# Attention reads its keys and values from a DRAM buffer of batch rows instead of by one gather per batch and source

## The reference, cut to what matters

```python
# x: 128 batches x 32 tokens x 256, that is 4096 tokens
x = x + ffn0(cond0(x))      # cond0: one of 200 matrices of 32x32 per batch; ffn0: 8 experts, top 2, low-rank terms
x = x + ffn1(attention(x))  # ffn1: 2 experts, top 1, hidden 1024

# attention: 8 heads in 4 groups, head size 32, paged cache of 4112 blocks of 16 positions
q, k, v = project(x); q, k = rope(rms(q)), rope(rms(k))
slot = pos // 16; off = pos % 16; blk = table[batch, slot]     # pos = kv_len + token
k_blocks[blk, :, off, :] = k;  v_blocks[blk, :, off, :] = v    # all batches write first
k_all = k_blocks[table]                                        # then all batches read
allowed = (kpos <= pos) & (kpos > pos - 128)                   # a window of 128 keys
o = softmax(where(allowed, q @ k_all.T / 16, -inf)) @ v_all
attention = o @ Wo.T
```

## Time and profile before

| what | value |
|---|---|
| median of 3 runs | 1223.65 us (1211.5 to 1227.43) |
| the profiled execution, its own time | 1226.37 us |
| its span, first to last instruction | 1224.6 us |
| PE / DVE / ACT / POOL busy | 945.7 / 721.4 / 535.9 / 559.1 us |
| mean granted clock of PE | 0.962 |
| moved by DMA | 130.04 MB |

### The profile page before, as it was taken

How to read it: one execution, slowest core, us unless ns; L and a number is a source line. 1 busy time by engine, 2 the same in 40 slices (tenths; PEclk the granted TensorE clock), 3 DMA queues, 4 the chain that set the end, 5 groups by cost and what they waited for, 6 DMA issues and landing times.

```text
span 1224.6 us, 21749 instructions
## 1 busy us (share of the span) xinstructions
PE 945.7 (77%) x4475; PEld 698.1 (57%) x4476; DVE 721.4 (59%) x2742; ACT 535.9 (44%) x1733; POOL 559.1 (46%) x558
## 2 busy tenths in 40 slices
PE   1896600789993766639988888888886999999995
PEld 1895400556662322218866677666774666767664
DVE  4225670344443899968978788878884444444442
ACT  0231000122221433329978787878783433333331
POOL 0001775050003777546777777777762122222221
PEclk9999999999997988968999999999997999999998
DMA  6766224874336644312222222222221111111110
GB/s 167 272 209 178 106 102 173 314 232 130 120 119 242 182 139 141 107 45 66 68 69 73 63 70 73 67 70 70 70 75 47 38 51 52 48 47 43 50 36 26
DMA packets 93174, 130.04 MB, mean 106 GB/s; under 512 B 28729, under 2 KB 77419, under 8 KB 91808
## 3 DMA queue, kind: packets, MB, share of 16 engines
q0 software_dynamic: 33872, 68.94, 18.9%
q1 hardware_dynamic: 44688, 42.02, 10.8%
q10 hardware_dynamic: 14576, 18.65, 5.0%
HBM read 98.37 MB, written 55.38 MB: 126 GB/s over the span
## 4 chain that ended last, share of the span: by engine, by line
PE 42%; issue 19%; POOL 19%; DMA 9%; DVE 8%; DVEq 1%; ACT 1%; SPq 0%; POOLq 0%; ACTq 0%
POOL kvring L417 12%; PE bank L839 9%; PE bank L851 9%; POOL slots_in L421 7%; PE bank L723 6%; PE bank L652 3%; DMA kvring<-written_blocks,read_i 2%; DMA work<-in_x 2%; PE bank L715 2%; PE bank L860 2%; PE bank L663 2%; DMA work<-slots_in 1%; DVE work L1153 1%; PE bank L731 1%; PE bank L770 1%
## 5 line engine op out<-in xcount | busy, mean ns | idle before, releaser
L421 POOL DMA_INDIRECT slots_in<-rows,slot_i x96 | 98.6, 1027 | 152.0 <-DVE slot_i L980 102.9
L417 POOL DMA_INDIRECT kvring<-in_cache,read_i x128 | 137.4, 1073 | 49.9 <-issue 36.0
L417 POOL DMA_INDIRECT kvring<-written_blocks,read_i x128 | 137.9, 1077 | 41.4 <-issue 40.8
L770 PE MATMUL bank<-work,kvring 88*128 88x256 f32 x512 | 136.0, 388 | 0.9 <-issue 0.8
L417 POOL DMA_INDIRECT work<-slots_out,slot_i x64 | 72.4, 1132 | 126.7 <-DMA slots_out<-work 102.4
L839 PE MATMUL bank<-experts,work 128*128 x264 | 126.4, 601 | 0.6 <-ACT work L621 0.6
L851 PE MATMUL bank<-experts,work 128*128 x528 | 124.9, 379 | 1.8 <-DVE work L1252 1.8
L851 PEld LDWEIGHTS bank<-experts,work 128*128 128x128 f32 x528 | 100.1, 190 | 43.2 <-issue 32.9
L421 POOL DMA_INDIRECT out_x<-work x33 | 33.2, 1007 | 191.2 <-DVE work L1264 178.4
L582 ACT ACTIVATE work<-work 128x176 f32<-128x176 f32 x256 | 110.3, 433 | 7.3 <-DVE work L1205 5.6
L1247 DVE TENSOR_TENSOR work<-bank,work 128x512 f32<-128x512 f32 x66 | 45.7, 692 | 106.4 <-ACT work L629 106.4
(11 more groups left out here) (235 smaller groups left out, 2016.2 us busy)
## 6 DMA issues: line engine op xcount, KB each, us to landing
slots_in<-work ACTq DMA_DIRECT2D x8, 1152.0 KB, 5.1
work<-slots_in SPq DMA_DIRECT2D x72, 128.0 KB, 2.1
slots_out<-work SPq DMA_DIRECT2D x72, 128.0 KB, 1.7
...
```

Source lines behind the costliest of these rows:

```text
L417: pool.indirect_dma_start(dst, None, src, bass.IndirectOffsetOnAxis(ap=index, axis=0), **kw).then_inc(done, 16)
L421: pool.indirect_dma_start(dst, bass.IndirectOffsetOnAxis(ap=index, axis=0), src, None, **kw).then_inc(done, 16)
L770: mm = pe.matmul(bank[6 + q // 2 % 2][:, (q % 2) * 256:(q % 2) * 256 + 256], kv[q][:, r * 256 + KW:r * 256 + 2 * KW], pt[q % 2][:, r * 256 ...
```

## The change

- **A buffer in DRAM.** Each group ("unit") of 8 batches gets a tensor `kv_rows` of 8 x 176 rows of 1 KB. `stage_cache(u)` gathers 88 whole blocks of 16 KB of the cache into one of two halves of `kvring`; `write_rows(u)` stores them. All 16 units are done in the first expert stage (`PRE2 = 16`), on POOL, unit `u` not before the share `u / 17` of the 72 tiles is done. They stand where the first 16 batch gathers stood, ahead of the gathers of the QKV stage.
- **The patch.** When the QKV stage has drained, `stage_copies(u)` gathers those of the 88 blocks that a batch has written to from `written_blocks`, and `write_copies(u)` scatters them over the buffer: four units at once, then one for each 8 batches, 32 batches ahead.
- **The read.** SP loads, for each batch, 160 consecutive rows (80 x 2 KB) from the buffer, starting at an offset that it reads into a register, into a ring of 16 batches in `work`. A window now has 160 keys and not 176.
- **PE.** Scores: four products, one for each group, 32 rows deep, 64 columns of weights, 160 columns (L837), in place of two of 128 x 128 x 176. Values: eight products with 32 columns of weights and 64 columns (L868) in place of two with 128 and 256. The keys of two batches are turned and copied together. The probabilities' turn is as before but for 80 in place of 88.
- **ACT and DVE.** ACT copies the turned probabilities (was DVE) and the output of a tile at once; the spreading of queries, the distance and the key copy leave it. DVE copies the keys of two batches at once, builds the mask in one instruction, and takes the minimum of scores that were scaled by -1/16 in the QKV stage, so that the bias needs no further instruction. POOL copies the queries of each tile into `cosine` (`queries`).
- **Lists.** The lists of blocks are made by three small matmuls with a constant of groups, in place of two turns.

```diff
--- before.py
+++ after.py
...
-KR = NR * BLK // 2
-NK = 2 * KR
+NK = WIN + T
+KR = NK // 2
+ROWS_B = NR * BLK
+PRE2 = 16
+GB = 8
 RING = 16
-AHEAD = 12
+NU = B // GB
+SB = GB * NR
...
+        kv_rows = [dram(f"kv_rows{u}_", [GB * ROWS_B, 2 * KW]) for u in range(NU)]
...
+        stage = [kvring[0:SB, k * 4096:k * 4096 + 4096] for k in range(2)]
+        kv = [work[0:KR, k * 512:k * 512 + 512] for k in range(RING)]
...
+            stage3_drained(sp)
+            for b in range(B):
+                u, j = b // GB, b % GB
+                if j == 0:
+                    sp.wait_ge(s4_rows[u % 2], 16 * (NU // 2 + u // 2 + 1))
+                wait(sp, s4_pv, b - RING + 1)
+                first = nc.s_assert_within(sp.value_load(first_i[0:1, b:b + 1]), 0, BLK - 1,
+                                           skip_runtime_bounds_check_because="an offset in a block")
+                sp.dma_start(kv[b % RING], kv_rows[u][bass.ds(first + j * ROWS_B, NK), :].rearrange(
+                    "(k r) f -> k (r f)", r=2)).then_inc(s4_in[b % RING], 16)
...
-            for b in range(RING):
-                gather(kv[b], cache_pairs, read_i[:, b:b + 1], s4_in[b], NPHYS * 8 - 1)
+            def entry(w, u):
+                return read_i[:, w * NU + u:w * NU + u + 1]
+
+            def kv_blocks(u):
+                return kv_rows[u].rearrange("(n r) f -> n (r f)", r=BLK)
+
+            def stage_cache(u):
+
+                wait(pool, s4_rows[u % 2], 16 * (u // 2))
+                gather(stage[u % 2], cache_blocks, entry(0, u), s4_stage[u % 2], NPHYS - 1)
+
+            def write_rows(u):
+
+                pool.wait_ge(s4_stage[u % 2], 16 * (u // 2 + 1))
+                pool.dma_start(kv_blocks(u), stage[u % 2]).then_inc(s4_rows[u % 2], 16)
+
+            def stage_copies(u):
+
+                pool.wait_ge(s4_rows[u % 2], 16 * (NU // 2 + u // 2))
+                gather(stage[u % 2], copies_list, entry(1, u), s4_stage[u % 2], NE * B - 1)
+
+            def write_copies(u):
+
+                pool.wait_ge(s4_stage[u % 2], 16 * (NU // 2 + u // 2 + 1))
+                scatter(kv_blocks(u), stage[u % 2], entry(2, u), s4_rows[u % 2], SB - 1)
+
+            for u in range(PRE2 + 1):
+                if u < PRE2:
+                    wait(pool, s2_d, u * N0 // (PRE2 + 1))
+                    stage_cache(u)
+                if u:
+                    write_rows(u - 1)
...
-            SCATTER_LAG = 32
-            for b in range(RING - AHEAD, B + RING - AHEAD):
-                if RING <= b < B:
-                    pool.wait_ge(s4_pv, b - RING + 1)
-                    gather(kv[b % RING], cache_pairs, read_i[:, b:b + 1], s4_in[b % RING], NPHYS * 8 - 1)
-                c0 = b - (RING - AHEAD)
-                pool.wait_ge(s4_in[c0 % RING], 32 * (c0 // RING) + 16)
-                gather(kv[c0 % RING], copies_pairs, read_i[:, B + c0:B + c0 + 1], s4_in[c0 % RING], NE * B * 8 - 1)
-                if b >= SCATTER_LAG and (b - SCATTER_LAG) % 4 == 0:
-                    scatter_tile((b - SCATTER_LAG) // 4)
-            for i in range((B + RING - AHEAD - 1 - SCATTER_LAG) // 4 + 1, NT):
-                scatter_tile(i)
+            def queries(tile):
+
+                wait(pool, s4_s, BT * (tile - 1))
+                pool.tensor_copy(qb[tile % 2].rearrange("p (b h t) -> p h b t", b=BT, h=2),
+                                 qt[:, tile * 256:tile * 256 + 256].rearrange("p (h b t) -> p h b t", h=2, b=BT)).then_inc(s4_qb, 1)
+
+            stage3_drained(pool)
+            pool.wait_ge(s3_tqc, NT)
+            for tile in range(2):
+                queries(tile)
+            for u in range(0, 4, 2):
+                for k in range(2):
+                    stage_copies(u + k)
+                for k in range(2):
+                    write_copies(u + k)
+            for s in range(B + 16):
+                u, tile = s // GB + 4, s // BT + 1
+                if s % GB == 0 and u < NU:
+                    stage_copies(u)
+                if s % GB == 5 and u < NU:
+                    write_copies(u)
+                if s % BT == 0 and 2 <= tile < NT:
+                    queries(tile)
+                if s % GB in (2, 4) and s >= 18:
+                    scatter_tile(2 * ((s - 18) // GB) + (s % GB == 4))
...
+            for st in skewed(act, B, 8, 2, 8):
                 if st.has(-1):
                     q = st.slot(-1) % 2
+                    act.wait_ge(s4_tp, st.s)
+                    wait(act, s4_pv, st.s - 2)
+                    act.activation(pt[q], tbank[0:KR, :], ACT.Copy).then_inc(s4_tpc, 1)
+                if st.q % 4 == 1 and st.has(-5):
+                    tile, t = 2 * st.turn(-5) + st.slot(-5) // 4, st.slot(-5) // 4
+                    act.wait_ge(s4_pv, BT * (tile + 1))
+                    act.activation(ot[t], vbank[t][:, 0:D], ACT.Copy).then_inc(s4_oc, 1)
+                if st.q % 4 == 3 and st.has(-7):
+                    tile, t = 2 * st.turn(-7) + st.slot(-7) // 4, st.slot(-7) // 4
+                    act.wait_ge(s4_w, tile + 1)
+                    act.activation(col(rows, tile * RW, D), vbank[t][:, D:2 * D], ACT.Copy).then_inc(s4_wc, 1)
+                if st.has(2):
+                    q = st.slot(2) % 2
+                    act.wait_ge(s4_ttr, 2 * (st.s + 3))
+                    wait(act, s4_pn, st.s + 1)
                     for g in range(2):
                         act.activation(pr[q][:, g * NK:g * NK + NK], sc[q][:, g * NK:g * NK + NK], ACT.Exp,
+                                       bias=mn[q][:, g:g + 1], scale=-1.0, accum_out=sm[q][:, g:g + 1]).then_inc(s4_ex, 1)
...
-            for w in range(2):
-                pe.transpose(bank[2][0:KR, P + w * B:P + w * B + B], read_b[:, w * KR:w * KR + KR], ident)
+            for w in range(3):
+                pe.matmul(bank[1][0:SB, 256 + w * NU:256 + (w + 1) * NU], lists[:, w * SB:w * SB + SB], c("group"),
+                          start=True, stop=True)
+            pe.matmul(bank[2][:, 2 * P:3 * P], c("ones"), diag[:, P:2 * P], start=True, stop=True)
...
+            for st in skewed(pe, B, 16, 4, 14):
...
+                if st.has(2):
+                    q, set_ = st.slot(2), st.slot(2) % 2
+                    t, tile, pair = q // 4 % 2, 4 * st.turn(2) + q // 4, 8 * st.turn(2) + q // 2
+                    pe.wait_ge(s4_ktc, pair + 1)
+                    if q % 4 == 0:
+                        pe.wait_ge(s4_qb, tile + 1)
+                    wait(pe, s4_ttr, 2 * (st.s + 1))
+                    for g in range(G):
+                        p0 = HD * g
+                        mm = pe.matmul(sbank[set_][g // 2][64 * (g % 2):64 * (g % 2) + 64, 0:NK],
+                                       qb[t][p0:p0 + HD, q % 4 * 64:q % 4 * 64 + 64],
+                                       kt[q // 2 % 2][p0:p0 + HD, (q % 2) * NK:(q % 2) * NK + NK], start=True, stop=True)
+                    mm.then_inc(s4_s, 1)
...
+                if st.has(-1):
+                    q, t, tile = st.slot(-1), st.slot(-1) // 4 % 2, 4 * st.turn(-1) + st.slot(-1) // 4
+                    pe.wait_ge(s4_tpc, st.s)
+                    if q % 4 == 0:
+                        wait(pe, s4_wc, tile - 1)
                     for r in range(2):
+                        for g in range(G):
+                            p0 = HD * g
+                            mm = pe.matmul(vbank[t][p0:p0 + HD, 0:D].rearrange("p (h b t) -> p b h t", h=2, b=BT)[:, q % 4, :, :],
+                                           kv[q][:, r * 256 + KW + p0:r * 256 + KW + p0 + HD],
+                                           pt[q % 2][:, r * 256 + 64 * g:r * 256 + 64 * g + 64], start=(r == 0), stop=(r == 1))
                     mm.then_inc(s4_pv, 1)
...
+                if st.has(0):
+                    q = st.q % 2
+                    pe.wait_ge(s4_pn, st.s + 1)
+                    wait(pe, s4_tpc, st.s)
...
-            dve.memset(work[:, 0:2048], 0.0).then_inc(s4_z, 1)
...
+                    pair, k = 4 * st.turn(4) + st.slot(4) // 2, st.slot(4) // 2 % 2
+                    dve.wait_ge(s4_kt, pair + 1)
+                    wait(dve, s4_s, 2 * pair - 2)
+                    dve.tensor_copy(kt[k], kbank[:, 0:2 * NK]).then_inc(s4_ktc, 1)
...
+                if st.has(3):
+                    q = st.slot(3) % 2
+                    wait(dve, s4_ttr, 2 * (st.s + 2))
+                    dve.scalar_tensor_tensor(out=pen[q], in0=c("before_key"), scalar=col(delta, st.s + 3), in1=c("outside"),
+                                             op0=ALU.add, op1=ALU.max).then_inc(s4_pen, 1)
```

289 lines of the change are left out of this document (114 added, 175 removed).

## The result

The changed kernel takes 1517.94 us (median of 4 runs, 1500.27 to 1524.5); the kernel before 1223.06 (median of 4). The ratio is 1.238, 95% interval 1.226 to 1.251: **slower by 24%, where 1250 and at most 1300 us were forecast**. The ratio is of fast runs alone and leaves out the changed kernel's 1524.5. The profiled execution took 1518.54 us, span 1516.7, mean granted clock 0.79.

A forecast was written before the change was run, and what follows sets the result against it. POOL's issue was taken to bound attention. The fill's delay of +66 us and -40 us to the second expert stage's start summed to +26, from the median 1223.65 to 1250 us; range 1190 to 1300.

The forecast's parts named there:

- What bounds the kernel before: Attention in the kernel before: POOL's issue of gathers and scatters was taken as the bound, 3.1 us a batch.
- The fill: Copying cache blocks to the buffer in the first expert stage: forecast to delay what follows by 66 us.
- 65.8 MB at 346 GB/s: Fill step: all DMA bytes from 257 us until QKV is under way, at that rate 190 us, to 447 us.
- 88 rows (11 engines): Fill rival: 88-row transfers use fewer engines; delay +90 us, pace 2.5, 1274 us in all; chance 0.15.
- The bound of +90: Upper bound of the fill's delay: 88 rows take as long as 128, 15.2 us a unit, ending at 480 us.
- The start: From the drain of QKV to the first keys turned: 16 us later than before, 10 to 22.
- The pace: Attention's time per batch: 2.5 us, from scores .55, values .90 and .15 of waiting beside PE's other work.
- the first rival: Attention: PE's small products run side by side, pace at the chain's 2.05 us, 1179 us in all; chance 0.22.
- Chain: ... 2.0 at the least: Attention: hand-overs between PE, ACT and DVE along one path over two batches allow 2.0 us a batch at the least.
- The tail: From the last keys turned to the second expert stage's first product: 27 us, difference forecast 0.
- the lists: Block lists by small matmuls, a few DVE and PE instructions ahead of stage two while POOL scatters: nothing.

The follow-up runs named there:

- e9: The kernel before, unchanged, run again with a profile: 1317 us, 1311 beside it; the changed kernel again, unchanged, in the same set: 1534 us.
- e3: Changed kernel with the fill's and patch's block transfers over 96 partitions in place of 88: 1451 us, kernel before beside it 1315.
- e7: Changed kernel with blocks that the patch writes anyway left out of the fill: 1430 us, kernel before beside it 1318.
- e14: Changed kernel with the first four units patched one by one, not two gathers then two scatters: 1497 us, kernel before beside it 1223.
- e10: Changed kernel with masking first, patched blocks left out, 96 partitions, first four units patched singly, 8 units filled early: 1306 us, kernel before 1311.
- e12: Changed kernel with masking first, patched blocks left out, 96 partitions, first patches single, 11 units filled early: 1254.47 us against the kernel before's 1223.01.
- e5: Changed kernel with DVE masking batch s+2 before normalising batch s+1: 1429 us, kernel before beside it 1318.
- e16: Changed kernel with PE turning the keys before Wo, DVE untouched: 1472 us, kernel before beside it 1313.

## Why the prediction was wrong

- **What bounds the kernel before** held: POOL's issue, 3.08 us a batch. e9 shows its condition, PE at a clock of 1.0.
- **The fill** failed by 85 of 151 us, the second largest part. The step that failed is "65.8 MB at 346 GB/s": the rate was of transfers over 128 partitions, and these had 88, which moved 233 GB/s. What the Trainium skill, "DMA: Bandwidth & Descriptors", section on why a DMA increments its semaphore by 16, says of 88 rows (11 engines) was weighed there at 0.15; the trace agrees, with 10 or 11 packets in flight, and e3 shows the effect. The bound of +90 was too low: it has a unit at 15.2 us, and it took 17.7, since a row held its engine 0.95 us and not 0.71. Also, bytes need not have moved at all: two thirds were written twice (e7).
- **The start**, 16 forecast, 35 measured: a patch's gather took 13 us against 8, its scatter 12 against 8, SP's read and the turn 13 against 3. The sizes had been taken from bytes alone. A gather takes 13 us with a second one in flight, 11 alone (e14), 9 alone over 96 partitions (e10, e12). What held SP's reads no run isolates.
- **The pace**, 2.5 forecast, 3.73 measured, 159 of the 268 us. What PE needs at full clock was sized too high, so the miss doesn't come from it. Here is the changed kernel in a stretch at full clock:

```profile
1060.05 0.43 PE L868 MATMUL bank<-wqkv_sb,work 80*32 80x64 f32 x16 [1.69 <-ACT wqkv_sb L648]
1060.41 0.63 PE L878 MATMUL bank<-cst,work 128*80 128x128 f32 x4
1060.97 0.50 PE L837 MATMUL bank<-route,cosine 32*64 32x160 f32 x8
1061.40 0.50 PE L857 MATMUL bank<-cst,work 80*128 80x80 f32 x4
1062.26 0.43 PE L868 MATMUL bank<-wqkv_sb,work 80*32 80x64 f32 x16 [0.36 <-ACT wqkv_sb L648]
```

  By starts, values take 0.36 us (forecast 0.90, one by one up to 1.7) and scores 0.43 (0.55): the small products do run side by side, the first rival's condition, the values too, which the forecast had nearly one by one. What failed is the step "Chain: ... 2.0 at the least". It followed one path through two batches and left out that DVE's masking stands behind the normalising, and this behind a copy that waits for PE behind Wo. Of the 85 steps from one batch's values to the next between 800 and 1100 us only five are near 2.0, at 2.2. The others with keys alone take 2.6 to 3.1, those with Wo or the router 3.8 to 5.3; and those in which PE has none of these still take 3.1 or 4.2, waiting for ACT's copy (906.73 to 909.84). e5 and e16 measure the circle, 0.79 and 0.45 a batch.
- **The clock** was in no term. It fell to 0.60, and in a stretch at the lower level PE needs 3.06 us for a step with keys (909.84 to 912.90), against 2.21 above, of which 0.36 are a wait. In part it is an effect: with the mask first it rose to 0.76 with the same products. That it's in part a cause is suggested by e10 and e12, in two sets. How much of the 3.73 is its own stays open, since no run has the changed kernel's order and products at a high clock.
- The tail and the lists were right, within 3.5 us.
